# Two-layer graph attention, layer 2: the context transposed by the vector engine and DRAM instead of the tensor engine, the output projection at the end of the pass, V one pass ahead

## What is computed

```
q, k = x @ Wq.T, x @ Wk.T;  v = x @ Wv.T + bv
scores = (q . k) * scale + (adj + adj);  p = softmax(scores)   # all-zero rows give 0
out = (p @ v) @ Wo.T + bo
x = layernorm(x + out)
```

## Time and profile before

| | us |
|---|---|
| median of 3 runs | 2070.93 (2070.71 to 2072.68) |
| the profiled execution, its own time | 2069.64 |
| its span, first to last instruction | 2067.8 |
| PE busy | 2028.7 (98%) |
| DVE busy | 1306.6 (63%) |
| ACT busy | 1137.7 (55%) |
| POOL busy | 514.5 (25%) |

### The profile page before, as it was taken

How to read it: one execution, slowest core, us unless ns; L and a number is a source line. 1 busy time by engine, 2 the same in 40 slices (tenths; PEclk the granted TensorE clock), 3 DMA queues, 4 the chain that set the end, 5 groups by cost and what they waited for, 6 DMA issues and landing times.

```text
span 2067.8 us, 46600 instructions
## 1 busy us (share of the span) xinstructions
PE 2028.7 (98%) x16832; PEld 1940.5 (94%) x16832; DVE 1306.6 (63%) x2430; ACT 1137.7 (55%) x2400; POOL 514.5 (25%) x625
## 2 busy tenths in 40 slices
PE   6999999999999999999999999998999999999997
PEld 6999999999999999999999999998899999999997
DVE  6655556655556655556655556655777767776775
ACT  6555555555555555545555555554556555655565
POOL 4223232223232223232223232222122212221221
PEclk9999999999999999999999999999999999999999
DMA  7122121122121121121121121122222222222221
GB/s 215 36 58 54 43 58 43 47 59 52 43 58 43 47 61 50 43 58 43 47 62 48 43 58 43 47 59 78 68 81 84 61 81 82 81 63 81 83 77 63
DMA packets 218876, 129.49 MB, mean 63 GB/s; under 512 B 129888, under 2 KB 217696, under 8 KB 218848
## 3 DMA queue, kind: packets, MB, share of 16 engines
q1 hardware_dynamic: 218848, 129.12, 23.1%
HBM read 78.40 MB, written 37.75 MB: 56 GB/s over the span
## 4 chain that ended last, share of the span: by engine, by line
PE 96%; DVE 2%; ACT 1%; DMA 0%; issue 0%; POOL 0%; SPq 0%; ACTq 0%; POOLq 0%; DVEq 0%
PE a_bank L328 59%; PE b_bank L1092 15%; PE b_banks L1092 5%; PE b_banks L1132 4%; PE a_bank L377 4%; PE b_bank L1155 2%; PE a_bank L404 2%; PE b_banks L1142 2%; PE a_bank L390 1%; PE b_bank L1165 1%; PE a_bank L414 1%; PE a_bank L431 1%; DMA a_work<-in_L_gnn_w 0%; DMA a_work<-in_L_gnn_wq 0%; DVE a_work L705 0%
## 5 line engine op out<-in xcount | busy, mean ns | idle before, releaser
L727 DVE TENSOR_TENSOR a_hid_lo<-a_work,a_hid_hi 128x512 fp32r<-128x512 f32 x192 | 146.6, 763 | 376.7 <-ACT a_hid_hi L573 376.7
L328 PE MATMUL a_bank<-a_x1t_hi,a_w_hi 128*128 128x256 f32 x1152 | 328.1, 285 | 1.5 <-DVE a_x1t_lo L713 1.5
L328 PE MATMUL a_bank<-a_x1t_lo,a_w_hi 128*128 128x256 f32 x1152 | 322.3, 280 | 0.0
L328 PE MATMUL a_bank<-a_x1t_hi,a_w_lo 128*128 128x256 f32 x1152 | 322.0, 280 | 0.0
L568 ACT ACTIVATE a_work<-a_bank,a_b 128x256 f32<-128x256 f32 x384 | 161.1, 472 | 283.5 <-PE a_bank L328 282.3
L919 POOL TENSOR_TENSOR a_work<-a_work,a_gamma 128x384 f32<-128x384 f32 x128 | 150.5, 1197 | 588.4 <-DMA a_work<-in_x 564.0
L328 PE MATMUL a_bank<-a_w_hi,a_hid_hi 128*128 128x384 f32 x768 | 264.1, 344 | 0.5 <-DVE a_hid_lo L727 0.5
L328 PE MATMUL a_bank<-a_w_lo,a_hid_hi 128*128 128x384 f32 x768 | 258.2, 336 | 0.0
L328 PE MATMUL a_bank<-a_w_hi,a_hid_lo 128*128 128x384 f32 x768 | 258.2, 336 | 0.0
L328 PEld LDWEIGHTS a_bank<-a_x1t_hi,a_w_hi 128*128 128x128 f32 x1152 | 217.8, 189 | 5.5 <-DVE a_x1t_lo L713 1.7
L328 PEld LDWEIGHTS a_bank<-a_x1t_lo,a_w_hi 128*128 128x128 f32 x1152 | 217.8, 189 | 0.0
(11 more groups left out here) (157 smaller groups left out, 5698.5 us busy)
## 6 DMA issues: line engine op xcount, KB each, us to landing
a_work<-in_x SPq DMA_DIRECT2D x64, 384.0 KB, 3.4
a_work<-in_xT SPq DMA_DIRECT2D x96, 128.0 KB, 2.6
x2T<-a_z_blocks SPq DMA_DIRECT2D x256, 48.0 KB, 1.7
x<-a_work SPq DMA_DIRECT2D x32, 384.0 KB, 2.7
b_xt_raw<-x2T SPq DMA_DIRECT2D x32, 384.0 KB, 3.5
b_res<-x SPq DMA_DIRECT2D x32, 384.0 KB, 3.8
out<-b_normed SPq DMA_DIRECT2D x32, 384.0 KB, 2.5
b_v_pairs<-b_v_nat SPq DMA_DIRECT2D x128, 49.5 KB, 2.0
```

The lines of the kernel that those rows point to most:

```text
L328: r = pe.matmul(out, lhs[a], rhs[b], start=first and n == 0, stop=last and n == 2)
L727: dve.tensor_tensor(hid[1][:, p % RING, :], silu[:, p % 2, :], hid[0][:, p % RING, :].bitcast(F32), ALU.subtract).then_inc(hid_lo, 1)
```

## The change

In layer 2 the six tensor-engine transposes per pass and their PSUM bank go. DVE transposes the context in 32x32 blocks (`turn_ctx`, two instructions per pass), SP stores the blocks in eight DMAs to a DRAM scratch (`store_ctx`), and one DMA of 384 KB brings them back re-placed (`load_ctxt`). The high and the low part of the turned context are then made by one ACT and one DVE instruction for the whole group instead of two each. The rows of the weight Wo are loaded in another order to suit (four DMAs instead of one, in layer 1's last pass). The orders of a pass become:

- PE: pv(b), scores(g), qk(g+1, 0 to 2), turn_p(g), values(g+1), attn_out(b).
- DVE: take_ctx(b), turn_ctx(b), soften(g) for both tiles, find_magnitude(g), take_k(g+1), ctxt_low(b), take_v(g+1), xt_low(g+2), finish(b).
- ACT: keep_v(g), square(g-2), take_q(g+1, 0), exp(g), norm(g-2), take_q(g+1, 1), take_pt(g), ctxt_high(b), xt_high(g+2).
- SP: load_res(b), store_ctx(b), swap_v(g), load_adj(g+1), load_ctxt(b), load_xt(g+2), store(g-2).
- POOL: as before.

```diff
def load_next():
...
-                for i, piece in enumerate(next_pieces):
+                for i, piece in enumerate(next_pieces[:3]):
...
+                rows_of = next_pieces[3][1].rearrange("(m k i) c -> m i k c", k=KT, i=32)
+                for m in range(4):
+                    sp.dma_start(stage(next_pieces[3])[32 * m:32 * m + 32], rows_of[m]).then_inc(next_loaded[3], 16)
...
             def step(g, att=True, ffn=True, late=True, more=True):
...
+        blocks, turned_raw = sb("b_blocks", [P, TILES, D]), sb("b_turned_raw", [P, TILES * D])
...
-        ctx_t = [sb(f"b_ctxt_{s}", [P, TILES, D], F32R) for s in ("hi", "lo")]
+        ctx_t = [sb(f"b_ctxt_{s}", [P, KT, GROUP], F32R) for s in ("hi", "lo")]
...
+            def store_ctx(g, t):
+                sp.wait_ge(ctx_turned, TILES * g + t + 1)
+                for s in range(P // 32):
+                    sp.dma_start(scratch["ctx"][P // 32 * t + s],
+                                 blocks[32 * s:32 * s + 32, t, :].rearrange("p (m c) -> p m c", m=4)).then_inc(ctx_stored, 16)
+            def load_ctxt(g):
+                sp.wait_ge(ctx_stored, 16 * N_TURNED * (g + 1))
+                sp.dma_start(turned_raw[:], scratch["ctxt"]).then_inc(ctxt_loaded, 16)
             def store(g):
...
+            load_xt(1)
+            def g_more(g):
+                return not isinstance(g, int) or g + 2 < NG
...
             def step(g, front=True, back=True, late=True, more=True):
-                if front and more:
-                    load_xt(g + 1)
+                if front and not back:
+                    sp.wait_ge(pairs_zeroed, 1)
...
-                if front and not back:
-                    sp.wait_ge(pairs_zeroed, 1)
+                    for t in range(TILES):
+                        store_ctx(g - 1, t)
...
+                if front and more:
+                    load_adj(g + 1)
+                if back:
+                    load_ctxt(g - 1)
+                if front and g_more(g):
+                    load_xt(g + 2)
...
-                if front and more:
-                    load_adj(g + 1)
...
-                elif u == 1:
+                else:
...
-                else:
-                    wait(pe, ctxt_lo, TILES * (g - 1))
...
             def values(g, t):
...
-                    wait(pe, ctxt_lo, TILES * (g - 1))
+                    wait(pe, v_done, TILES * (g - 1) + 1)
...
-                    pe.wait_ge(pt_done, TILES * (g - 1) + t + 1)
+                    wait(pe, y_done, TILES * (g - 2) + t + 1)
...
             def turn_p(g, t):
...
-                wait(pe, y_done, TILES * (g - 1) + t + 1)
...
+                else:
+                    pe.wait_ge(ctx_done, TILES * g)
...
-            def turn_ctx(g, t, front):
-                pe.wait_ge(ctx_done, TILES * g + t + 1)
-                if front and t == 0:
-                    pe.wait_ge(v_done, TILES * (g + 1) + 1)
+            def attn_out(g, t, front):
+                pe.wait_ge(ctxt_lo, g + 1)
+                if front:
+                    pe.wait_ge(pt_done, TILES * (g + 1) + t + 1)
...
-                    r = pe.transpose(one[TURN_BANK[t]][:, k * P:(k + 1) * P], ctxt[:, t, k * P:(k + 1) * P], ident[:])
-                r.then_inc(ct_mm, 1)
-            def attn_out(g, t, front):
-                pe.wait_ge(ctxt_lo, TILES * g + t + 1)
-                if front:
-                    pe.wait_ge(biased, TILES * (g + 1) + t + 1)
-                for k in range(KT):
-                    r = mm3(two[t][:, 0:D], [ctx_t[j][:, t, k * P:(k + 1) * P] for j in range(2)],
+                    r = mm3(two[t][:, 0:D], [ctx_t[j][:, k, t * P:(t + 1) * P] for j in range(2)],
...
+            for t in range(TILES):
+                values(0, t)
...
             def step(g, front=True, back=True, more=True):
...
-                if front:
-                    for t in range(TILES):
-                        values(g, t)
...
+                if front and more:
+                    for u in range(3):
+                        qk(g + 1, u)
+                if front:
+                    for t in range(TILES):
+                        turn_p(g, t)
+                if front and more:
+                    for t in range(TILES):
+                        values(g + 1, t)
...
-                        turn_ctx(b, t, front)
-                if front and more:
-                    qk(g + 1, 0)
-                if back:
-                    for t in range(TILES):
...
-                if front and more:
-                    qk(g + 1, 1)
-                    qk(g + 1, 2)
-                if front:
-                    for t in range(TILES):
-                        turn_p(g, t)
...
-            def ctxt_high(g, t):
-                act.wait_ge(ct_mm, TILES * g + t + 1)
-                wait(act, o_mm, TILES * (g - 1) + t + 1)
-                act.activation(ctx_t[0][:, t, :], one[TURN_BANK[t]][:, 0:D], ACT.Copy).then_inc(ctxt_hi, 1)
+            def ctxt_high(g):
+                act.wait_ge(ctxt_loaded, 16 * (g + 1))
+                wait(act, o_mm, TILES * g)
+                act.activation(ctx_t[0][:].rearrange("p k (n j) -> p k n j", j=32),
+                               turned_raw[:].rearrange("p (n k j) -> p k n j", k=KT, j=32), ACT.Copy).then_inc(ctxt_hi, 1)
...
             def square(g, t):
...
+            xt_high(1)
+            def g_more(g):
+                return not isinstance(g, int) or g + 2 < NG
...
             def step(g, front=True, back=True, late=True, more=True):
...
-                if front and more:
-                    xt_high(g + 1)
...
-                if back:
-                    for t in range(TILES):
-                        ctxt_high(b, t)
...
+                if front:
+                    for t in range(TILES):
+                        exp(g, t)
...
-                if front:
-                    for t in range(TILES):
-                        exp(g, t)
...
+                if back:
+                    ctxt_high(b)
+                if front and g_more(g):
+                    xt_high(g + 2)
...
-            with act.Fori(2, NG - 1) as g:
+            with act.Fori(2, NG - 2) as g:
...
+            step(NG - 2)
...
-                wait(dve, ct_mm, TILES * (g - 1) + t + 1)
...
-            def ctxt_low(g, t):
-                dve.wait_ge(ctxt_hi, TILES * g + t + 1)
-                dve.tensor_tensor(ctx_t[1][:, t, :], one[TURN_BANK[t]][:, 0:D], ctx_t[0][:, t, :].bitcast(F32),
+            def turn_ctx(g, t):
+                dve.wait_ge(ctx_done, TILES * g + t + 1)
+                if t == 0:
+                    wait(dve, ctx_stored, 16 * N_TURNED * g)
+                dve.transpose(blocks[:, t, :], ctxt[:, t, :]).then_inc(ctx_turned, 1)
+            def ctxt_low(g):
+                dve.wait_ge(ctxt_hi, g + 1)
+                dve.tensor_tensor(ctx_t[1][:].rearrange("p k (n j) -> p k n j", j=32),
+                                  turned_raw[:].rearrange("p (n k j) -> p k n j", k=KT, j=32),
+                                  ctx_t[0][:].bitcast(F32).rearrange("p k (n j) -> p k n j", j=32),
...
             def finish(g):
...
+            for t in range(TILES):
+                take_v(0, t)
+            xt_low(1)
+            def g_more(g):
+                return not isinstance(g, int) or g + 2 < NG
...
             def step(g, front=True, back=True, late=True, more=True):
...
+                if back:
+                    for t in range(TILES):
+                        take_ctx(b, t)
+                    for t in range(TILES):
+                        turn_ctx(b, t)
...
-                        take_v(g, t)
+                        soften(g, t)
+                    for t in range(TILES):
+                        find_magnitude(g, t)
+                if front and more:
+                    take_k(g + 1)
...
-                    for t in range(TILES):
-                        take_ctx(b, t)
+                    ctxt_low(b)
...
-                    xt_low(g + 1)
-                if front:
-                    soften(g, 0)
-                if back:
-                    for t in range(TILES):
-                        ctxt_low(b, t)
-                if front:
-                    soften(g, 1)
-                    for t in range(TILES):
-                        find_magnitude(g, t)
+                    for t in range(TILES):
+                        take_v(g + 1, t)
+                if front and g_more(g):
+                    xt_low(g + 2)
...
-                if front and more:
-                    take_k(g + 1)
...
-            with dve.Fori(2, NG - 1) as g:
+            with dve.Fori(2, NG - 2) as g:
...
+            step(NG - 2)
...
-            step(NG + 1, front=False, back=False)
...
+    ctx_turned = nc.dram_tensor("ctx_turned", (P, TILES * D), F32).ap()
+    scratch = {"ctxt": ctx_turned, "ctx": ctx_turned.rearrange("(m i) (s c) -> s i m c", i=32, c=D // 4)}
```

(27 more changed lines are left out.)

## The result

The changed kernel takes 2118.23 us (median of 4 runs, 2117.65 to 2121.1), the kernel before 2071.15: a ratio of 1.0227, 95% interval 1.0214 to 1.0241. The forecast was 2116 us, in a range of 2085 to 2150. The profiled execution took 2117.65 us with a span of 2115.8, which is 48.0 more than the span before.

The account below looks back on a forecast made before the run. PE alone bounded the kernel; the new order would make it wait 1.6 us a pass. 24.9 + 6.8 + 10.6 + 3.0 = 45.3 on 2069.64 = 2114.9; median 1.3 above: 2116 us, range 2085 to 2150.

Parts of the forecast that it names:

- ahead of the first back: Layer 1 and the first pass of layer 2: only the loading of Wo changes, under cover; zero.
- passes 1 to 30: Layer 2's steady passes: each takes 19.7 us instead of 18.87, in all +24.9 us.
- pass 31, clock included: Pass 31, without next group's V and qk as cover: +6.8 us, with the clock's fall +8.3.
- last pass to the last y, clock included: Last pass, from p @ v to last y, nothing overlapping: +10.6 us, with the clock's fall +12.1.
- The ring: Dependences from a pass's first p @ v (T) through DVE, POOL, ACT to the output projection: next pass at T + 19.7.
- PE's saving: The six transposes leave PE: 0.81 us less a pass, so PE alone would need 18.06 us.
- The way through DRAM: Context stores, then load_ctxt issued at T + 10.9 and landed at T + 14.4, hidden behind ACT's 14.6.
- 0.2 to spare: Margin in us between the context load landing (T + 14.4) and ACT being free for ctxt_high (T + 14.6).
- The upper bound in the prediction, T + 15.9: Latest landing of the context load, with slower stores and a slower load; the pass would be 21.0 us.
- Rival 3: The context load lands after ACT is free: 2155 us at T + 15.9, 2135 likelier; chance 0.18.
- rival 4: The clock falls in every pass when PE stalls: up to 45 us more, up to 2161; chance 0.04.
- The tail: Pass 31 and the last pass, short of cover: +6.8 and +10.6 us, plus 3.0 for the lowered clock.

Follow-up runs that it names:

- no_turn: The changed kernel without its two DVE transposes per pass, the context going to DRAM as it is; 2089.44 us, ratio 1.0080.
- both_early: The changed kernel with the moves of both load_early and norm_early; 2081.69 us, ratio 1.0053.
- load_early: The changed kernel with the turned context's load issued right behind its stores, ahead of the four swaps of V and the bias load; 2116.54 us, ratio 1.0218.
- norm_early: The changed kernel with ACT's normalisation of group g-2 moved from behind the exponentials to ahead of take_q(g+1, 0); 2112.36 us, ratio 1.0186.
- tail_on_pe: xt_first with the context of the last two groups turned by the tensor engine as before; 2045.90 us, ratio 0.9872.
- xt_first: q_late with the load of the inputs of group g+2 ahead of the context's stores in SP's queue; 2066.37 us, ratio 0.9976.
- q_late: both_early with take_q(g+1, 1) on ACT moved from ahead of take_pt to behind ctxt_high; 2079.66 us, ratio 1.0042.

## Why the prediction was right

The 48.0 us between the two spans, term by term:

| term | forecast | measured | from |
|---|---|---|---|
| ahead of the first back | 0 | +2.1 | 1474.52 against 1476.61 |
| passes 1 to 30 | +24.9 | +26.3 | 2069.11 - 1476.61 = 592.5, against 566.2 |
| pass 31, clock included | +8.3 | +8.4 | 20.63 against 12.21 |
| last pass to the last y, clock included | +12.1 | +11.2 | 18.38 against 7.20 |

(1474.52 is the start of the first p @ v in the kernel before.) The 2.1 us ahead of layer 2 are already there at layer 1's first turned result (100.76 against 98.64 us), whose code the change does not touch. In the traces of the nine other kernels, with the same code up to there, it comes between 98.68 and 103.14 us: a difference of executions, not an effect.

**The ring** held in each of its steps (as distances from T = 1774.09):

| | forecast | measured |
|---|---|---|
| first reciprocal | 1.0 | 1.11 |
| transposes begin, end of their DVE time | 3.1, 4.05 | 3.00, 3.95 |
| maximum of tile 1 | 6.9 | 6.75 |
| exp(g, 1) | 9.5 | 9.38 |
| ctxt_high | 14.6 | 14.40 |
| output projection | 16.55 | 16.32 |
| next pass | 19.7 | 19.65 |

The last step hides two small errors that cancel: the projection started 0.2 us sooner and took 3.33 to the next pass, not 3.13.

Its two supports were tried apart: no_turn shortened DVE's part and the pass followed; both_early shortened ACT's part and the pass followed; load_early left ACT's part alone and nothing moved. PE's saving was real as well: with the ring out of the way, the pass is 18.05 us.

**The way through DRAM** was cheaper by 0.4 than I had it (load issued at T + 10.52, not 10.9): eight stores take SP 3.64 us and not the 4.24 of layer 1's, and the swaps and the bias load give 0.3 of that back. The timeline of SP's queue:

```profile
1777.68 3.64 SPq L1056 DMA_DIRECT2D ctx_turned<-b_blocks  x8
...
1784.61 0.39 SPq L1061 DMA_DIRECT2D b_turned_raw<-ctx_turned  x1
```

With the median landing of 3.5 us, the "0.2 to spare" became 0.4, and norm_early shows that distance from the other side. (The upper bound in the prediction, T + 15.9, is a slip: its own terms add up to 15.7.)

**Rival 3 and rival 4** are not the case, but each occurs in single passes. In seven of the 30 the load landed after ACT was free and released ctxt_high; six of these cost at most 0.35 us each. The seventh is 21.72 us long (1693.31 to 1715.03). There the load landed 4.41 us after issue, PE paused for 1.8 us, and the clock fell. Busy time per engine and granted clock, changed kernel:

```profile
1708.00:1710.00 2.00, 0.31 (x2) 0.00 (x0) 0.86 (x1) 1.47 (x2) 0.00 (x0) 1.00 0.50 184
1710.00:1712.00 2.00, 1.85 (x6) 1.85 (x7) 1.90 (x4) 0.22 (x1) 0.00 (x0) 0.60 0.00 0
1712.00:1714.00 2.00, 2.00 (x8) 2.00 (x8) 0.56 (x2) 0.00 (x0) 0.00 (x0) 0.54 0.00 0
```

That pass (2.1 over the others), and a few tenths of late landing, at full clock, in the passes that start at 1476.61, 1496.42 and 1852.70, make the 30 passes 26.3 and not 30 x 0.78 = 23.4. The forecast's 24.9 lies between the two and has no term for them: part of its closeness is luck. The forecast told rival 4 from its own case by a pause near 2.5 us; that was wrong, for here the clock fell after 1.8, and rival 4 had less distance than I gave it. By the rule of the Trainium skill cited ahead (Perfetto Trace Analysis, Matmul Optimizations: matmuls back to back, power by utilization) such a fall is to be looked for in each pass with a pause; the trace agrees in one pass of 30 and not in the others.

**The tail** came out within 1 us in sum, and within 0.1 in pass 31, but there by luck. The chain of waits in pass 31, then in the last pass:

```profile
2079.03 3.08 DMA b_turned_raw<-ctx_turned
...
2084.02 5.79 PE b_banks L1116 x18
...
2098.12 3.27 DMA b_turned_raw<-ctx_turned
...
2103.30 4.79 PE b_banks L1116 x18
```

The load was issued 0.5 us sooner than forecast and landed 0.4 faster, so that the projection of pass 31 started at T + 14.9, not 15.9; the lower clock level then cost it 2.4 us (5.79 against 3.42 in a steady pass), where 1.5 was forecast. In the last pass the clock cost 1.4 and the way to the projection was 0.9 shorter. tail_on_pe shows the tail from the other side: 20.5 us less than xt_first.

What the forecast did not have is that the reordered pass has a second ring, through xt_low and finish, which stood just behind the first and set the pass of q_late.

## What to carry to other kernels

Work taken from the bound engine pays only if what replaces it fits under the cover that remains: write the new order of each engine down, follow the one ring that goes through the moved result, and compare its length with the bound engine's sum before any code is written. Where two waits end within a few tenths of one another, edit them together, for each alone shows nearly nothing. And a pipeline's last passes have no cover: keep the short path there, even if the long one is right for all the others.

## What the runs showed of the hardware

- The granted clock fell after a pause of only 1.8 us in PE (last matmul at 1707.97 with 0.34, next at 1710.15; then 0.60 and 0.54), while the pauses of 1.2 to 1.7 us in the other steady passes left it full. The length of the pause does not decide it alone: in norm_early the clock fell after pauses of 1.77, 1.80, 1.94, 2.26 and 2.67 us and stayed full after one of 1.88 (the pass that starts at 1680.06). What else decides was not tried. In pass 31 and the last the projection at the lower level took 5.79 and 4.79 us instead of 3.42.
- A DVE subtraction of 128x384 with both inputs in SBUF took up to 1831 ns beside a POOL subtraction, against 547 with one input in PSUM. By the Trainium skill (GPSIMD Engine Reference, Specifications) POOL shares its SBUF interfaces with DVE and contends with DVE instructions that have two SBUF inputs; the trace agrees. POOL's subtraction, which the first ctxt_low overlaps, took 1.64 us instead of 1.48. In the changed kernel ctxt_low has two SBUF inputs too, but takes 957 to 960 ns for 768 elements; POOL is idle there.
- A load of 384 KB from DRAM, the same in each pass, landed 3.0 to 4.4 us after issue in the changed kernel and up to 4.8 in norm_early, where SP issues another load of 384 KB right behind it; in load_early, where the small swaps of V follow it, it landed after 3.0 to 3.5. That the neighbour makes the spread was not tried by itself.
